# Loads of the scan's first inputs moved into the stage before it, and the last row store waited for by its readers

## The reference, cut to what matters

```
x = x + L0_xattn(layernorm(x), fside, ctx)         # int8-like linears: quantise, multiply, silu gate
x = x + L0_ffn(layernorm(x), lut, idx)             # gate, up, down weights looked up in a 16-entry table
x = x + L1_xattn(ctx, layernorm(x), ...)           # selective scan over time, gated by silu(layernorm(x))
x = x + L1_ffn(layernorm(x), ...)                  # 32 experts, top 8

# the scan of L1_xattn, per batch; 512 channels, 16 states, 512 steps
state = state * exp(dt[..., None] * A) + (dt * u)[..., None] * B[:, None, :]
y     = sum_n state[n] * C[n] + D * u
```

## Time and profile before

| what | value |
|---|---|
| median of 3 runs | 1883.29 us (1882.07 to 1884.48) |
| the profiled execution, its own time | 1881.68 us |
| its span, first to last instruction | 1879.5 us |
| mean granted TensorE clock in it | 0.897 of full speed |
| busy: TensorE matmul, VectorE, ScalarE, GpSimd | 83%, 70%, 48%, 42% of the span |
| moved by DMA | 445 MB, mean 237 GB/s |

### The profile page before, as it was taken

One profiled execution on the slowest core, in us unless ns is written; L12 is line 12 of the kernel. 1 busy time (PEld: TensorE's weight loads), 2 busy tenths in 40 slices (PEclk: granted clock), 3 DMA queues, 4 the chain that ended last, 5 costly groups with the idle time before them and its releaser, 6 DMA issues. The chain is left out here.

```text
span 1879.5 us, 26432 instructions
## 1 busy us (share of the span) xinstructions
PE 1554.0 (83%) x9418; PEld 1319.2 (70%) x9426; DVE 1308.7 (70%) x1901; ACT 911.0 (48%) x1577; POOL 791.8 (42%) x481
## 2 busy tenths in 40 slices
PE   5857778677528987996898799975899999999896
PEld 3444355454428976895897689855789999999785
DVE  6677586786659989999998999642445555555452
ACT  3444545445234444344444534432466666666463
POOL 1010000010045456445655643177735766762555
PEclk9878888888758997997999799987999999999998
DMA  7988799984682492375359236379998999999876
GB/s 213 343 281 275 274 321 368 333 270 157 210 314 95 175 357 74 119 283 222 106 188 370 82 118 218 145 266 338 382 365 232 250 269 253 256 260 223 226 170 85
DMA packets 187942, 445.48 MB, mean 237 GB/s; under 512 B 41616, under 2 KB 43664, under 8 KB 177568
## 3 DMA queue, kind: packets, MB, share of 16 engines
q1 hardware_dynamic: 115040, 283.37, 44.7%
q0 software_dynamic: 31760, 74.48, 16.8%
q10 hardware_dynamic: 41008, 85.89, 12.6%
HBM read 246.77 MB, written 205.28 MB: 241 GB/s over the span
## 5 line engine op out<-in xcount | busy, mean ns | idle before, releaser
L1441 POOL TENSOR_TENSOR mix_st<-mix_Bb,mix_du 128x2048 f32<-128x2048 f32 x64 | 293.3, 4583 | 268.2 <-DVE mix_st L2225 255.7
L2217 DVE TENSOR_TENSOR_SCAN mix_st<-mix_YY,mix_st 128x512 f32<-128x512 f32 x256 | 312.0, 1219 | 46.0 <-POOL mix_st L1441 24.0
L1895 ACT ACTIVATE mix_YY<-mix_dt,mix_A 128x512 f32<-128x512 f32 x256 | 176.9, 691 | 276.5 <-DVE mix_st L2217 272.3
L1492 POOL DMA_INDIRECT out_x<-moe_ys,moe_meta x130 | 210.5, 1619 | 190.1 <-ACT moe_ys L2032 84.6
L1611 PE MATMUL mix_G<-mix_xThi,mix_wup 128*128 128x256 f32 x1408 | 273.0, 291 | 14.5 <-issue 13.6
L1611 PEld LDWEIGHTS mix_G<-mix_xThi,mix_wup 128*128 128x128 f32 x1408 | 231.8, 199 | 17.6 <-issue 16.2
L1793 PE MATMUL mix_Dp<-moe_xhi,moe_whi 128*128 128x288 f32 x768 | 234.5, 305 | 2.0 <-ACT moe_xhi L1995 1.5
L1793 PE MATMUL mix_Dp<-moe_xhi,moe_wlo 128*128 128x288 f32 x768 | 228.9, 298 | 0.0
L1793 PE MATMUL mix_Dp<-moe_xlo,moe_whi 128*128 128x288 f32 x768 | 228.7, 298 | 0.0
L2357 DVE TENSOR_TENSOR moe_xlo<-mix_G,moe_xhi 128x512 fp32r<-128x512 f32 (+1 forms) x160 | 102.2, 638 | 170.5 <-ACT moe_xhi L1995 167.9
L1637 PE MATMUL mix_YY<-mix_ident,mix_st 128*128 128x128 f32 x1024 | 145.1, 296 | 86.2 <-DVE mix_st L2225 86.2
(11 more groups left out here) (237 smaller groups left out, 3064.9 us busy)
## 6 DMA issues: line engine op xcount, KB each, us to landing
x_by_expert<-front_zeros ACTq DMA_DIRECT2D x16, 4480.0 KB, 24.1
mix_wup<-w_halves SPq DMA_DIRECT2D x44, 1024.0 KB, 5.5
moe_raw<-in_ew SPq DMA_DIRECT2D x32, 1280.0 KB, 8.5
moe_xt<-x_by_expert SPq DMA_DIRECT2D x128, 256.0 KB, 8.6
mix_wdn<-w_halves SPq DMA_DIRECT2D x44, 512.0 KB, 6.4
front_idx<-in_idx SPq DMA_DIRECT2D x44, 384.0 KB, 9.0
w_halves<-front_wst SPq DMA_DIRECT2D x44, 384.0 KB, 7.9
mix_Bb<-bc_rows SPq DMA_DIRECT2D x16, 1024.0 KB, 9.4
```

What stands on the lines that cost most here:

```text
L1441: nc.gpsimd.tensor_tensor(st[:, g % STBUF, :, :], Bb[:, q, :, :], du[:, k % 2, :].unsqueeze(1).to_broadcast([P, NG, S]), ALU.mult).then_in ...
L1492: pool.indirect_dma_start(out=out_rows, out_offset=bass.IndirectOffsetOnAxis(ap=meta[0:rows, e % MBUF, j, 0:1].bitcast(U32), axis=0), in_= ...
L1895: nc.scalar.activation(dA, dt[:, k % 2, :], ACT.Exp, scale=A[:, c, m:m + 1]).then_inc(da_ready, 1)
L2217: nc.vector.tensor_tensor_scan(r, dA, r, 0.0, ALU.mult, ALU.add).then_inc(scanned, 1)
```

## The change

SyncE no longer waits for stores at the end of the first block, except for `filled`. Readers of X1 wait instead: `load_x` for the batch that it loads, and the first residual for all four, since its result overlays the buffer of the last store. The wait for the BC, U, DT and DU stores moves to the new `load_ahead`, called at slot 170 of 176, which issues there the loads of dt and du of column 0, of all four groups of `Bb`, and of the rows of batch 0. These four tiles are allocated outside both blocks. For this the first block's buffers get fixed places: those that are alive at slot 170 are kept off the places of these tiles, and `xt` is split in two. In the second block these loads are gone, GpSimd does `inputs_product(0)` before its memsets and identity matrix, and ScalarE and VectorE no longer wait for `pool_made`. The first copy of y waits for the weight stores, whose staging buffer it overlays. Two semaphores are saved by letting others count further.

```diff
@@ constants
+AHEAD_AT = 170
+AHEAD_LOADS = 7
+STATE_AT = 18560
+HALF_AT = 157824
+DT_AT = 166016
+Y_AT = 186496
+XT_AT = 202880
@@ front_block, buffers
+        sb = Place(nc, "front_", STATE_AT, STATE_AT + 32768)
+        v = sb("v_all", [P, DC, S], F32)
+        e = sb("e_all", [P, DC, S], F32)
+        w1 = sb("w1_all", [P, DC, S], F32)
+        u = sb("u_all", [P, DC, S], F32)
...
+        sb = Place(nc, "front_", XT_AT + 8192, LAST_BYTE)
+        wsT = sb("wsT", [P, DC, S], F32)
+        xt1 = sb("xt1", [P, TT, D], F32)
+        xt = (xt0, xt1)
+        Bb, dt, du, xt_mix = ahead
@@ front_block, SyncE
+            def load_ahead():
+                sp.wait_ge(bc_out, 16 * NB)
+                sp.wait_ge(u_out, 16 * NB)
+                sp.wait_ge(dt_out, 32 * NB)
+                sp.dma_start(dt[:, 0, :], s["DT"][0][:, 0, :]).then_inc(ahead_in, 16)
+                sp.dma_start(du[:, 0, :], s["DU"][0][:, 0, :]).then_inc(ahead_in, 16)
+                for q in range(GROUPS):
+                    sp.dma_start(Bb[:, q, :, :], s["BC"][0][NG * q:NG * q + NG, :].unsqueeze(0).to_broadcast([P, NG, S])
+                                 ).then_inc(ahead_in, 16)
+                sp.dma_start(xt_mix[:, 0, :, :], s["X1"][0].rearrange("(t p) n -> p t n", p=P)).then_inc(ahead_in, 16)
+
             for t in range(SLOTS + 8):
                 b, o = divmod(t, PER_BATCH)
                 pb, po = divmod(t, TURN)
+                if t == AHEAD_AT:
+                    load_ahead()
...
-            sp.wait_ge(bc_out, 16 * NB)
-            sp.wait_ge(u_out, 16 * NB)
-            sp.wait_ge(dt_out, 32 * NB)
-            sp.wait_ge(x1_out, 16 * NB)
             sp.wait_ge(filled, 16 * (FILLS + 2))
@@ mix_and_experts_block, SyncE
             def load_x(b):
                 if b > 1:
                     sp.wait_ge(x3_ready, b - 1)
+                sp.wait_ge(x1_out, 16 * b + 16)
...
-            load_column(0, 0)
-            load_b(0, 0)
             load_c(0, 0)
-            load_x(0)
-            load_b(0, 1)
             load_c(0, 1)
             load_up(0)
             load_down(0)
             for q in (2, 3):
-                load_b(0, q)
                 load_c(0, q)
@@ GpSimd
+            inputs_product(0)
             nc.gpsimd.memset(eps[:, :], EPS).then_inc(pool_made, 1)
...
@@ ScalarE
             act.wait_ge(const_in, 32)
-            act.wait_ge(pool_made, 5)
...
                 act.wait_ge(unit_done, GROUPS * k + GROUPS)
+                if b == 0:
+                    for q in range(2):
+                        act.wait_ge(w_out[q], 32 * CH)
@@ VectorE
-            dve.wait_ge(pool_made, 5)
...
                     dve.wait_ge(half_done, HALVES * b + HALVES)
+                    if b == 0:
+                        dve.wait_ge(x1_out, 16 * NB)
```

More of the change, by code:

```diff
@@ L150, in batch_at, with front_block @@
     return b if o == 0 and 0 <= b < NB else -1
-def front_block(nc, d, s, filled, w_out):
+def front_block(nc, d, s, filled, w_out, x1_out, ahead_in, ahead):
     with ExitStack() as ctx:
-        def sb(name, shape, dt):
-            return ctx.enter_context(nc.sbuf_tensor("front_" + name, shape, dt))
         def sem(name):
             return ctx.enter_context(nc.semaphore("front_" + name))
+        sb = Place(nc, "front_", FIRST_BYTE, STATE_AT)
         ident = sb("ident", [P, P], F32)
@@ L729, in moments @@
                 for t in range(TT):
-                    last = nc.vector.bn_stats(stats[:, t, :], xt[:, b % 2, t, :])
+                    last = nc.vector.bn_stats(stats[:, t, :], xt[b % 2][:, t, :])
                 link(last)
@@ L959, in downs_of_slot, with mix_and_experts_block @@
     return early + halves_of_slot(g - 2)
-def mix_and_experts_block(nc, d, s, out, filled, w_out):
+def mix_and_experts_block(nc, d, s, out, filled, w_out, x1_out, ahead_in, ahead):
     ALL = NB * UNITS
@@ L995, in mix_and_experts_block @@
         nmr = few("nmr", [P, 3, TT], F32)
-        sb = Place(nc, "mix_", state_at, weight_at)
-        Bb = sb("Bb", [P, GROUPS, NG, S], F32)
+        Bb, dt, du, xt = ahead
+        sb = Place(nc, "mix_", state_at + 32768, weight_at)
         Cb = sb("Cb", [P, GROUPS, NG, S], F32)
@@ L1179, in mix_and_experts_block, with wait_column @@
         MERGE = DEFER + 1 + -(-LATE_TILES // LATE_PER)
+        def wait_column(eng, k):
+            if k == 0:
+                eng.wait_ge(ahead_in, 16 * AHEAD_LOADS)
+            else:
+                eng.wait_ge(dt_du_in[k % 2], 32 * (k // 2) + 32 * (k % 2))
         def stored(q, n):
@@ L1420, in _, with inputs_product @@
         def _(pool):
+            link = Link(pool, pool_link)
+            def inputs_product(g):
+                b, l = divmod(g, UNITS)
+                c, q = divmod(l, GROUPS)
+                k = DC * b + c
+                wait_column(pool, k)
+                if b > 0:
+                    pool.wait_ge(b_in[q], 16 * b)
+                if g >= STBUF:
+                    pool.wait_ge(unit_done, g - STBUF + 1)
+                if g >= 2:
+                    pool.wait_ge(prod_ready, 2 * (g - 1))
+                nc.gpsimd.tensor_tensor(st[:, g % STBUF, :, :], Bb[:, q, :, :],
+                                        du[:, k % 2, :].unsqueeze(1).to_broadcast([P, NG, S]),
+                                        ALU.mult).then_inc(dbu_ready, 1)
+            inputs_product(0)
             nc.gpsimd.memset(eps[:, :], EPS).then_inc(pool_made, 1)
@@ L2384, in _ @@
                 if l == 0:
-                    dve.wait_ge(x_in[b % 2], 16 * (b // 2) + 16)
+                    if b == 0:
+                        dve.wait_ge(ahead_in, 16 * AHEAD_LOADS)
+                    else:
+                        dve.wait_ge(x_in[b % 2], 16 * (b // 2) + 16 * (b % 2))
                     moments(0, xt[:, b % 2, :, :], (0, 1))
@@ L2538, in build @@
         w_out = [whole.enter_context(nc.semaphore(f"w_out{q}")) for q in range(2)]
-        front_block(nc, d, s, filled, w_out)
-        mix_and_experts_block(nc, d, s, out, filled, w_out)
+        x1_out = whole.enter_context(nc.semaphore("x1_out"))
+        ahead_in = whole.enter_context(nc.semaphore("ahead_in"))
+        ahead = (Place(nc, "mix_", STATE_AT, STATE_AT + 32768)("Bb", [P, GROUPS, NG, S], F32),
+                 Place(nc, "mix_", DT_AT, DT_AT + 4096)("dt", [P, 2, S], F32),
+                 Place(nc, "mix_", DT_AT + 4096, DT_AT + 8192)("du", [P, 2, S], F32),
+                 Place(nc, "mix_", XT_AT, XT_AT + 16384)("xt", [P, 2, TT, D], F32))
+        front_block(nc, d, s, filled, w_out, x1_out, ahead_in, ahead)
+        mix_and_experts_block(nc, d, s, out, filled, w_out, x1_out, ahead_in, ahead)
 def lay_out(inputs):
```

84 lines of the change are left out of this document (33 added, 51 removed).

## The result

The changed kernel takes 1863.99 us, the median of four runs (1860.04 to 1865.49), beside 1882.88 us, the median of four runs of the kernel before. The ratio, estimated from all these runs and not the quotient of the two medians, is 0.9895, interval [0.9878, 0.9913]; by it the kernel before's 1882.88 us become 1863.1. The profiled execution took 1865.08 us around a span of 1863.3 us; the sum of the prediction made it 1865.4. So the profiled executions differ by 1881.68 - 1865.08 = 16.6 us, where 16.3 was said, and the medians by 18.9 us. The prediction had 1867.0 us for the median and 1863.5 to 1871.5 as its range.

The account below looks back on a forecast made before the run. VectorE was taken to bound the scan stage and TensorE the experts, with both idle between 509 and 533 us. Gains of 14.5 + 1.15 + 0.66 = 16.3 us gave a median of 1867.0 us, range 1863.5 to 1871.5.

Parts of the forecast that it names:

- Start of the second block: SyncE at the first block's end: without the X1 wait, the second block starts at 513.4 instead of 519.57, 6.2 us.
- The constants decide: Before the first scan: A and dskip land behind X1 at 517.3, plus 1.35 us; scan at 518.7, 14.5 us earlier.
- The lower bound: Second block's start: constants land 1.8 us after issue, about 515.6, so GpSimd's product decides; first scan at 518.0.
- Two stalls behind it: Early scan stage: long first product with Cb loses 1.15 us, the wait for u 0.66 us.
- The early loads: Seven loads, 5.5 MB, issued from slot 170: land by 503.5 at the latest, wanted at 513.4, 10 us of cover.
- Nothing comes back: Scan stage: what is won before the first scan is kept, since VectorE's waits there are all for ScalarE.
- Disturbance of the first stage: Rival: early loads delay the last index half, VectorE up to 13.5 us late, leaving 2.8 us, 1880.5; 5 in 100.
- slower one-hots by the fixed places: Rival, first stage: fixed buffer places slow 176 one-hots; at 0.12 us more each, 1888 us; 4 in 100.
- a loss later on: Rival, scan stage: a wait for a weight load or TensorE takes back about half, 1875; 5 in 100.
- The rival of late loads: Rival, second block's start: Bb lands at, say, 517, first scan at 521.6; gain 13.4 us, 1870; 8 in 100.
- More than I count: Rival: a stall of the scan's first units or of the experts' start goes too, 1862; 5 in 100.
- the three terms: Gains summed: first scan 14.5 us earlier, first product with Cb 1.15, wait for u 0.66; 16.3 us.

Follow-up runs that it names:

- loads_only: Changed kernel, but SyncE again waits for the X1 store at the end of the first block; 1871.62 us, ratio 0.9943 to the kernel before.
- collide: Changed kernel with six small memsets delaying GpSimd's second product, so it runs beside VectorE's first product with Cb; 1866.47 us, ratio 0.9928.
- wait_only: Changed kernel with the early loads put back into the second block in their old order, the X1 wait still removed; 1876.2 us, ratio 0.9969.
- again: The changed kernel run once more, no edit; 1863.21 us, ratio 0.9901 to the kernel before.
- again2: The changed kernel run once more on another, slower chip, no edit; 1927.23 us, ratio 0.9923 to the kernel before there.
- pool_order: Changed kernel with GpSimd's set-up instructions ahead of its first product again, as in the kernel before; 1864.01 us, ratio 0.9915.
- consts_ahead: Changed kernel with the constants A and dskip also loaded ahead, at slot 170 of the first block; 1865.2 us, ratio 0.9904.
- product_ahead: Changed kernel with constants loaded ahead, and A and GpSimd's first product made in the first block; 1862.15 us, ratio 0.9901.
- product_ahead2: Changed kernel with constants loaded ahead, A and GpSimd's first product made in the first block, on the slower chip; 1920.64 us, ratio 0.9895.
- before_again: The kernel before run again on the first chip for a second trace, no edit; 1882.89 us, ratio 1.0.
- before_third: The kernel before run again on another, slower chip for a third trace, no edit; 1943.99 us, ratio 1.0013.

## Where the prediction failed, and what of it was right

The mechanism came out as told, and the gain in the changed stretch too; the time of the runs did not, and the step that failed stands behind this list. The numbers of the steps, in distances that the drift of the first stage doesn't touch:

- *Start of the second block.* From the last add to the block's first issue: 519.57 - 506.92 = 12.65 us before, 513.67 - 507.30 = 6.37 after: 6.3 us, where 6.2 was said.
- *The constants decide.* dskip landed at 517.98, 0.4 us behind X1, where I took some 0.15 from the stores of 1 MB. From there to the scan 1.35 us (said 1.35). D1 shrank by 26.29 - 12.03 = 14.3 us, where 14.5 was said; the difference is this landing. The lower bound would have been right for loads with no store ahead of them, as in loads_only. The rule of the Trainium skill ("DMA: Bandwidth & Descriptors", on queues, rings and completion order) pointed the right way, but I had read more into it than it states. It orders the writes of one DMA engine, and the section itself says that completion is not first in, first out per issuing engine. The trace agrees: dskip landed 0.4 us behind the store, but A, the load issued first, 0.4 us ahead of the store's own end. So the 517.15 us of the prediction was no bound for the constants, nor 518.5 one for the first scan. Both took about twice the 1.8 us of the empty queue.
- *Two stalls behind it.* D2 shrank by 2.0 us more than D1 (16.3 against 14.3), where 1.15 + 0.66 = 1.81 was said. The product with Cb took 1.19 instead of 2.37 us, the idle time 0.76 instead of 1.42, together 1.84. collide shows the first of them alone.
- *The early loads* landed at 508.0, not at 503.5. I had divided 5.5 MB by 416 GB/s from the end of the fill. These MB are of 1024 KB, so the quotient is 13.9 us and not 13.2. The fill ended at 467.33 + 24.3 = 491.6, and from 491 to 508 us the DMA engines moved 363 GB/s and not 416, 6.2 MB, in which the two stores of half 20 (384 KB each, from 497.28) are counted. So the cover was 5.7 us and not 10. It sufficed; the one-hots and the X1 store came 0.4 us later than before, which is within the drift of the table. By these numbers, an estimate, loads longer by more than 5.7 us would begin to lose one for one.
- *Nothing comes back.* From the first scan to the last it took 642.4 us before and 640.5 after, 1.9 us less, which the two stalls (1.84) account for.
- *The rivals.* Disturbance of the first stage or slower one-hots by the fixed places, beyond the drift of 1 to 2 us, and a loss later on are excluded by the rows above. The rival of late loads put its limit at 240 GB/s, as the mean of a stretch in which half the time nothing was queued; the DMA engines were busy for 72% of it. *More than I count* had 1862, and the median came nearer to it than to 1867.0. But the stall that it asks for isn't seen: behind the first scan only the two stalls that were counted are gone, and the experts' stage of after, 703.4 us, is that of before, 703.8. SyncE's 12.81 us from 497.28 hold 10.6 us of waiting for ScalarE's evictions, and it was back for X1.

**The step that failed is the last one: from the gain in the trace to the median of the runs.** I cost everything outside the three terms at nothing, laid the new median 1.6 us above the profiled execution as in the kernel before, which gave 1867.0, and took the spread of three runs of the kernel before, 2.4 us, for all the scatter in the range. The three terms measured 16.3 us, as summed. But the medians differ by 18.9 us: 1863.99 us is 3.0 under the forecast, and the 1863.1 us of the ratio are under the lower end of the range. Of the extra 2.6 us, 2.3 are where the profiled executions lie among the runs: that of before 1.2 us under its kernel's median, that of after 1.1 us above. The other 0.3 is between the two profiled executions, and it is outside the span. A run's time exceeds its span, first to last instruction, by 2.2 to 2.3 us in the executions of the kernel before and by 1.7 to 1.8 us in those of the changed one, so that 0.4 us of the gain repeats there. It is 1.8 us in loads_only and 2.2 in wait_only, but 2.1 in collide, which has the loads ahead too; what it hangs on stays open. To see whether they belong to the kernel I set, for every kernel beside the runs of before on its chip, the gain in D2 beside the difference of medians. D2 of before is 60.36 for after, 60.3 otherwise on chip 1, and 60.14 on chip 2:

| kernel | gain in D2 | gain in medians | difference |
|---|---|---|---|
| after | 16.3 | 18.9 | 2.6 |
| again | 16.3 | 20.2 | 3.9 |
| again2 | 16.1 | 14.5 | -1.6 |
| pool_order | 16.2 | 17.8 | 1.6 |
| consts_ahead | 17.3 | 18.2 | 0.9 |
| loads_only | 11.2 | 11.8 | 0.6 |
| wait_only | 5.0 | 7.2 | 2.2 |
| collide | 15.4 | 15.4 | 0.0 |
| product_ahead | 20.3 | 19.7 | -0.6 |
| product_ahead2 | 20.1 | 21.1 | 1.0 |

The differences are of both signs, with a mean of 1.1 us, of which the 0.4 us outside the span is a part. Two groups of runs of the very same kernel before differ by 1.1 us (1882.89 and 1881.83) and 2.3 us (1943.99 and 1941.69). So most of the excess looks like scatter, and the traces show it in two places: the first stage, whose last add lies between 506.05 and 508.27, and the experts, between 701.8 and 706.5 us on chip 1. Of the experts' times there, the two of the kernel before have a mean of 705.2, the eight of the other kernels 703.1; on chip 2 it is the kernel before that is lowest. That is too few traces to tell a gain of 2 us from none. In the first stage one thing that varies is seen. TensorE's two matmuls ahead of VectorE's last four steps, in the timelines of after and of product_ahead:

```profile
500.26 1.02 PE L568 MATMUL front_Q<-front_dg,front_ones 128*128 128x512 f32 x2
```

```profile
499.40 1.91 PE L581 MATMUL front_Q<-front_dg,front_ones 128*128 128x512 f32 x2
```

The pair took 0.9 us longer in the second, and VectorE's idle time behind it was 5.31 us instead of 4.10. The longer form is also in again, again2, before_again, before_third, loads_only, wait_only and product_ahead2, so it goes with no edit. Nor does it set where the stage ends: again has it, and the earliest last add of all. Beyond the 0.4 us, the mean excess over ten pairs that share their runs of before can't be told from nothing here; whether another part of a us is real stays open. The 16.3 us are shown, by three traces of the changed kernel, one of them on another chip.

## What to carry to other kernels

A wait at a block's end can be worth less than its length when the next block's loads go on the same queue as the transfer that was waited for: in wait_only 6.2 us of earlier start gave 5.0 us. What is issued behind the store should be nothing that the next step needs at once, the smallest constants included: 1.1 us here. Most of the gain, 11.2 of 16.3 us, comes from issuing the large loads before it. And for an edit of under 1% measure a distance between two events around it in the trace, which repeated within 0.22 us here, where medians of 11 to 17 runs of one kernel differed by 1.1 and 2.3 us.

## What was not expected of the hardware

- The issue of a 2 KB load took 1.34 and 1.36 us with a 1 MB store unfinished on its queue, and 0.42 us on an empty one. SyncE's loads behind it start later by that, though they need nothing of it. The issue of A just ahead of it took 0.34 to 0.35 us either way.
- One chip ran the experts' stage 60 us longer, 8%, for all three kernels, with the scan stage unchanged. Windows of before_again and, below, of before_third, columns as in the earlier trace rows:

```profile
1176.00:1881.00 705.00, 638.34 (x4161) 564.50 (x4159) 342.48 (x655) 378.20 (x706) 408.92 (x303) 0.95 0.89 247
570.00:1170.00 600.00, 526.69 (x3709) 490.65 (x3709) 561.81 (x734) 274.79 (x499) 319.14 (x111) 0.92 0.51 186
```

```profile
1176.00:1937.00 761.00, 651.10 (x4163) 572.78 (x4161) 342.02 (x655) 377.14 (x706) 407.18 (x303) 0.92 0.83 229
570.00:1170.00 600.00, 523.66 (x3707) 488.24 (x3707) 561.60 (x734) 274.04 (x499) 319.73 (x111) 0.93 0.51 186
```

The instructions are the same in both. TensorE, at a granted clock of 0.92 instead of 0.95, is busy 12.8 us longer, too little for the 56 us between these stretches; DMA moves 229 GB/s instead of 247. The cause was not looked for. A time from one chip is therefore not set beside one of another, only ratios and distances are.
